# Loading the first quad's attention operands from inside the projection's program, with the projection unrolled

## What is computed

```python
q, k, v = split_heads(x @ Wq.T + bq), split_heads(x @ Wk.T + bk), split_heads(x @ Wv.T + bv)
q, k = rope(q), rope(k)
att = softmax(where(tril, q @ k.T / sqrt(16), -inf))
x = layernorm(x + (att @ v) @ Wo.T + bo)
h = silu(lin(x, w1)) * lin(x, w2)
h = gelu(lin(h, h1)); h = gelu(lin(h, h2))
out = layernorm(x + lin(h, w3))
```

## Time and profile before

| | |
|---|---|
| median of the three runs | 3086.01 us |
| profiled execution, its time | 3089.17 us |
| profiled execution, its span | 3087.4 us |
| TensorE matmuls busy | 2862.5 us (93%) |
| VectorE busy | 2063.2 us (67%) |
| ScalarE busy | 1302.7 us (42%) |
| GpSimd busy | 95.5 us (3%) |
| mean granted TensorE clock | 0.964 |

### The profile page before, as it was taken

The page is one execution under the profiler, slowest core; times in us unless marked ns, Lnnn a source line. Parts: engine busy times, 40 slices in busy tenths (PEclk is TensorE's granted clock), DMA queues, the critical chain, the costliest instruction groups (busy, mean ns, idle before and its releaser), DMA issues. The chain is left out here.

```text
span 3087.4 us, 40615 instructions
## 1 busy us (share of the span) xinstructions
PE 2862.5 (93%) x15648; PEld 1514.1 (49%) x15648; DVE 2063.2 (67%) x3638; ACT 1302.7 (42%) x2545; POOL 95.5 (3%) x122
## 2 busy tenths in 40 slices
PE   8949999999999989999999994699999994999998
PEld 4423333333333323333333332477777773888887
DVE  7979999887776779998877743655444432334333
ACT  0005666777777656667777772111111110010110
POOL 0030200020000200000000000000000000000000
PEclk9969999999999989999999997799999997999999
DMA  5541440034000440000000003211111004111200
GB/s 161 153 91 34 65 54 5 5 48 58 5 5 9 62 58 5 5 4 5 5 5 5 5 12 97 77 55 51 54 54 54 34 31 155 69 41 41 82 14 21
DMA packets 86620, 138.35 MB, mean 45 GB/s; under 512 B 27744, under 2 KB 57312, under 8 KB 83776
## 3 DMA queue, kind: packets, MB, share of 16 engines
q1 hardware_dynamic: 72352, 92.06, 9.2%
q0 software_dynamic: 5472, 23.34, 6.1%
q10 hardware_dynamic: 8640, 20.85, 2.1%
HBM read 85.22 MB, written 50.99 MB: 44 GB/s over the span
## 5 line engine op out<-in xcount | busy, mean ns | idle before, releaser
L506 DVE TENSOR_REDUCE at_segmax<-at_row 128x1 f32<-128x512 f32 (+3 forms) x2304 | 1330.3, 639 | 260.5 <-PE at_row L436 193.2
L559 ACT ACTIVATE at_probs<-at_key 128x512 f32<-128x512 f32 (+3 forms) x2304 | 1136.8, 567 | 546.8 <-PE at_key L452 376.8
L436 PE MATMUL at_row<-at_k_stack,at_q_stack 96*128 96x512 bf16 (+3 forms) x2304 | 814.7, 372 | 33.8 <-POOL at_values L362 28.7
L452 PE MATMUL at_key<-at_q_stack,at_k_stack 99*128 99x512 bf16 (+3 forms) x2304 | 814.3, 366 | 20.8 <-DMA at_q_stack<-maxima 11.7
L471 PE MATMUL at_o<-at_probs,at_values 128*32 128x512 f32 (+2 forms) x4608 | 574.7, 571 | 0.0
L436 PEld LDWEIGHTS at_row<-at_k_stack,at_q_stack 96*128 96x128 bf16 x2304 | 223.5, 99 | 595.1 <-DVE at_segmax L506 406.2
L452 PEld LDWEIGHTS at_key<-at_q_stack,at_k_stack 99*128 99x128 bf16 x2304 | 224.6, 98 | 279.2 <-ACT at_probs L559 129.4
L1012 PE MATMUL na_h<-na_h_h,na_h2w_h 128*128 128x512 f32 x512 | 203.5, 397 | 45.9 <-DVE na_h_l L1065 45.9
L1050 ACT ACTIVATE na_h3f<-na_h,na_hs 128x512 f32<-128x512 f32 x64 | 44.0, 688 | 442.0 <-PE na_h L1012 442.0
L746 PE MATMUL wi_f<-wi_h_h,wi_h1w_h 128*128 128x512 f32 x512 | 207.3, 405 | 10.4 <-DVE wi_h_l L877 10.4
L1012 PE MATMUL na_h<-na_h_h,na_h2w_l 128*128 128x512 f32 x512 | 203.2, 397 | 0.0
(11 more groups left out here) (108 smaller groups left out, 2520.9 us busy)
## 6 DMA issues: line engine op xcount, KB each, us to landing
hidden<-wi_h SPq DMA_DIRECT2D x64, 256.0 KB, 2.0
na_h2f<-hidden SPq DMA_DIRECT2D x8, 2048.0 KB, 8.6
at_q_stack<-q_parts POOLq DMA_DIRECT2D x72, 128.0 KB, 23.7
at_k_stack<-k_parts POOLq DMA_DIRECT2D x18, 512.0 KB, 28.4
outputs<-at_outs SPq DMA_DIRECT2D x32, 256.0 KB, 2.0
wi_o<-outputs SPq DMA_DIRECT2D x8, 1024.0 KB, 5.9
q_parts<-pr_parts SPq DMA_DIRECT2D x48, 128.0 KB, 1.9
k_parts<-pr_parts SPq DMA_DIRECT2D x48, 128.0 KB, 2.3
```

Of the source, the lines that this page charges most:

```text
L436: last = nc.tensor.matmul(bank[:, 0:w], qst[u][0:SROWS, c, h, i * P:(i + 1) * P], kst[u][0:SROWS, h, s * CH:s * CH + w], start=True, stop= ...
L452: last = nc.tensor.matmul(bank[:, q0:CH], kst[u][0:SROWS + PARTS, h, j * P:(j + 1) * P], qst[u][0:SROWS + PARTS, c, h, q0:CH], start=True, ...
L506: nc.vector.tensor_reduce(segmax[:, n % 2, h * TPC + i, s:s + 1], row_ps[r % RING_R][:, 0:w], op=ALU.max, axis=AX.X).then_inc(rows_taken, 1)
L559: nc.scalar.activation(probs[:, g % RING_P, h, q0:CH], key_ps[m % RING_K][:, q0:CH], ACT.Exp).then_inc(probs_ready, 1)
```

## The change

The tiles of the first quad (stacks, values, the float32 constants) move into a class `First`, allocated around both programs. In the projection:

* the hardware loops of ACT, PE, DVE and SP are written out for all eight chunks; the semaphores are no longer given their first counts ahead, the first waits are left out instead;
* SP issues the two constants first of all, and `load_first(n - 1)` in chunk n behind the stores of q and of the first half of the values. It first waits for all stores of chunks up to n - 1, and issues thirteen DMAs (six for the query stack, six for the key stack, one for the values of that chunk, 136 KB). `load_first(7)` stands at the end, behind the wait for all stores;
* POOL fills the ones and the pad of the first quad's tiles behind the staging tile.

In the attention SP has no loads of stacks left, POOL fills only the second buffer's pad and ones and then waits for chunk 7 of the first quad, and goes on to the loads of quad 1. PE waits for one pad, and for the values of quad 0 chunk by chunk.

```diff
         @block.gpsimd
         def _(pool):
             nc.gpsimd.memset(vals[:, :, :, :, :], 1.0).then_inc(v_ones, 1)
+            pool.wait_ge(v_ones, 1)
+            nc.gpsimd.memset(first.kst[SROWS:SROWS + PARTS, :, :], 1.0).then_inc(v_ones, 1)
+            pool.wait_ge(v_ones, 2)
+            nc.gpsimd.memset(first.vq[:, NT * QUAD * VW:], 0.0).then_inc(v_ones, 1)
+            pool.wait_ge(v_ones, 3)
...
         @block.sync
         def _(sp):
...
+            def load_first(n):
+
+                for s in range(2):
+                    sp.wait_ge(parts_stored[s], 96 * (n + 1))
+                    sp.wait_ge(v_stored[s], 32 * (n + 1))
+                for r, (qa, ka) in enumerate(TERMS):
+                    part = slice(r * HD, (r + 1) * HD)
+                    sp.dma_start(first.qst[part, n, :, :], q_v[qa, 0, :, n]).then_inc(first.loaded[n], 16)
+                    sp.dma_start(first.kst[part, :, n * CH:(n + 1) * CH], k_v[ka, 0, :, n]).then_inc(first.loaded[n], 16)
+                sp.dma_start(first.vq[:, n * TPC * QUAD * VW:(n + 1) * TPC * QUAD * VW],
+                             v_d[0, :, n].rearrange("p i e -> p (i e)")).then_inc(first.loaded[n], 16)
+
+            sp.dma_start(first.ident32[:, :], io["ident"]).then_inc(first.consts_loaded, 16)
+            sp.dma_start(first.mask32[:, :], io["mask"]).then_inc(first.consts_loaded, 16)
+            for n in range(NCH):
+                for i, dst in enumerate((qp_d, kp_d)):
+                    for half in range(DH):
+                        m = PAIRS * n + DH * i + half
+                        sp.wait_ge(parts_ready, 2 * m + 2)
+                        for a in range(PARTS):
+                            sp.dma_start(dst[a, half * P:(half + 1) * P, n, :],
+                                         parts[:, half, a, :]).then_inc(parts_stored[half], 16)
+                    sp.wait_ge(v_taken, 2 * n + i + 1)
+                    for j in range(2):
+                        sp.dma_start(v_d[:, :, n, 2 * i + j, :].rearrange("q p e -> p q e"),
+                                     vals[:, i, j, :, :].rearrange("p (q h) e -> p q (h e)", q=NQUAD)
+                                     ).then_inc(v_stored[i], 16)
+                    if n > 0 and i == 0:
+                        load_first(n - 1)
+            load_first(NCH - 1)
...
@@ attend, POOL
-            load_values(0, 0)
-            for u in range(2):
-                nc.gpsimd.memset(vq[u][:, NT * QUAD * VW:], 0.0).then_inc(pad_ready, 1)
-                pool.wait_ge(pad_ready, u + 1)
-                nc.gpsimd.memset(kst[u][SROWS:SROWS + PARTS, :, :], 1.0).then_inc(ones_ready[u], 1)
-                pool.wait_ge(ones_ready[u], 1)
-            pool.wait_ge(first_loaded[NCH - 1], 12 * 16)
+            nc.gpsimd.memset(vq[1][:, NT * QUAD * VW:], 0.0).then_inc(pad_ready, 1)
+            pool.wait_ge(pad_ready, 1)
+            nc.gpsimd.memset(kst[1][SROWS:SROWS + PARTS, :, :], 1.0).then_inc(ones_ready, 1)
+            pool.wait_ge(ones_ready, 1)
+            pool.wait_ge(first.loaded[NCH - 1], 13 * 16)
             load(1, 1)
             load_values(1, 1)
...
@@ attend, SP
-            load_first(0)
-            sp.dma_start(ident32[:, :], io["ident"]).then_inc(consts_loaded, 16)
-            sp.dma_start(mask32[:, :], io["mask"]).then_inc(consts_loaded, 16)
-            for c in range(1, FIRST_AHEAD):
-                load_first(c)
...
                             store_max(n)
-                            if n + FIRST_AHEAD < NCH:
-                                load_first(n + FIRST_AHEAD)
...
@@ attend, DVE
-            dve.wait_ge(consts_loaded, 32)
-            nc.vector.tensor_copy(ident[:, :], ident32[:, :]).then_inc(consts_ready, 1)
-            nc.vector.tensor_copy(mask[:, :], mask32[:, :]).then_inc(consts_ready, 1)
+            dve.wait_ge(first.consts_loaded, 32)
+            nc.vector.tensor_copy(ident[:, :], first.ident32[:, :]).then_inc(consts_ready, 1)
+            nc.vector.tensor_copy(mask[:, :], first.mask32[:, :]).then_inc(consts_ready, 1)
```

More of the change, by code:

```diff
@@ L54, with project @@
 EPS = 1e-5
-def project(nc, io, qp_d, kp_d, v_d):
+def project(nc, io, qp_d, kp_d, v_d, first):
     with ExitStack() as ctx:
@@ L119, in _ @@
             load(1, 1)
-            with act.Fori(0, NCH // 2 - 1) as it:
-                for u in range(2):
-                    act.wait_ge(v_ready, it * 4 + 2 * u + 2)
-                    act.wait_ge(pair_taken, it * 2 * PAIRS + PAIRS * (u + 1) + 2)
-                    load(u, it * 2 + (2 + u))
+            for n in range(2, NCH):
+                act.wait_ge(v_ready, 2 * (n - 2) + 2)
+                act.wait_ge(pair_taken, PAIRS * (n - 1))
+                load(n % 2, n)
         @block.gpsimd
@@ L133, in _ @@
             pe.wait_ge(weights_ready, 6)
[L134 to L150, removed]
+            for n in range(NCH):
+                u = n % 2
+                pe.wait_ge(x_loaded[u], 16 * (n // 2 + 1))
+                for i, (w, wr) in enumerate(((wq, wqr), (wk, wkr))):
+                    for half in range(DH):
+                        m = PAIRS * n + DH * i + half
+                        cols = slice(half * P, (half + 1) * P)
+                        if m >= 2:
+                            pe.wait_ge(pair_taken, m - 1)
+                        for bank, weight in ((main_ps[half], w), (rot_ps[half], wr)):
@@ L156, in _ @@
+                    for j in range(2):
+                        tile = slice((2 * i + j) * P, (2 * i + j + 1) * P)
+                        for c in range(DH):
+                            last = nc.tensor.matmul(v_ps[i][:, j, :], xt[:, u, c, tile], wv[:, c, :],
+                                                    start=(c == 0), stop=(c == DH - 1))
+                    last.then_inc(v_ready, 1)
         @block.vector
         def _(dve):
-            dve.sem_inc(pair_taken, 2)
-            dve.sem_inc(v_taken, 2)
@@ L176, in _ @@
             dve.wait_ge(v_ones, 1)
[L177 to L212, removed]
@@ L214, in _ @@
         @block.sync
         def _(sp):
[L216 to L232, removed]
@@ L233, in _ @@
[L233 to L235 removed]
+            q_v = qp_d.rearrange("a (q h d) n t -> a q d n h t", q=NQUAD, d=HD)
+            k_v = kp_d.rearrange("a (q h d) n t -> a q d n h t", q=NQUAD, d=HD)
+            def load_first(n):
[8 more added lines that the diff above has]
+                             v_d[0, :, n].rearrange("p i e -> p (i e)")).then_inc(first.loaded[n], 16)
@@ L284, in rows_before_keys, with __init__, sb, attend @@
     return before
-def attend(nc, io, qp_d, kp_d, v_d, max_d, o_d):
+class First:
+    def __init__(self, nc, ctx):
+        def sb(name, shape, dt=F32):
+            return ctx.enter_context(nc.sbuf_tensor("fi_" + name, shape, dt))
+        self.qst = sb("q_stack", [P, NCH, QUAD, CH], BF16)
+        self.kst = sb("k_stack", [P, QUAD, T], BF16)
+        self.vq = sb("values", [P, NT * QUAD * VW + 32 - VW])
+        self.ident32 = sb("ident32", [P, P])
+        self.mask32 = sb("mask32", [P, P])
+        self.loaded = [ctx.enter_context(nc.semaphore(f"fi_loaded{c}")) for c in range(NCH)]
+        self.consts_loaded = ctx.enter_context(nc.semaphore("fi_consts_loaded"))
+def attend(nc, io, qp_d, kp_d, v_d, max_d, o_d, first):
     blocks, rows, groups = attend_plan()
@@ L304, in sem @@
             return ctx.enter_context(nc.semaphore("at_" + name))
-        qst = [sb(f"q_stack{u}", [P, NCH, QUAD, CH], BF16) for u in range(2)]
-        kst = [sb(f"k_stack{u}", [P, QUAD, T], BF16) for u in range(2)]
-        vq = [sb(f"values{u}", [P, NT * QUAD * VW + 32 - VW]) for u in range(2)]
+        qst = [first.qst, sb("q_stack1", [P, NCH, QUAD, CH], BF16)]
+        kst = [first.kst, sb("k_stack1", [P, QUAD, T], BF16)]
+        vq = [first.vq, sb("values1", [P, NT * QUAD * VW + 32 - VW])]
         probs = sb("probs", [P, RING_P, QUAD, CH])
         outs = sb("outs", [P, 2, CH])
-        ident32 = sb("ident32", [P, P])
-        mask32 = sb("mask32", [P, P])
         ident = sb("ident", [P, P], BF16)
@@ L465, in values @@
                     pe.wait_ge(out_taken, n)
-                if j == 0 and n % NCH == 0:
+                if j == 0 and quad == 0:
+                    pe.wait_ge(first.loaded[c], 13 * 16)
+                elif j == 0 and n % NCH == 0:
                     pe.wait_ge(values_loaded[quad], 16)
@@ L484, in _ @@
                             if quad == 0:
-                                pe.wait_ge(first_loaded[c], 12 * 16)
+                                pe.wait_ge(first.loaded[c], 13 * 16)
                             elif m % NCH == 0:
@@ L1137, in build @@
     h2_d = nc.dram_tensor("hidden2", [NCH, P, FK, CH], F32, kind="Internal").ap()
-    project(nc, io, qp_d, kp_d, v_d)
-    attend(nc, io, qp_d, kp_d, v_d, max_d, o_d)
+    with ExitStack() as ctx:
+        first = First(nc, ctx)
+        project(nc, io, qp_d, kp_d, v_d, first)
+        attend(nc, io, qp_d, kp_d, v_d, max_d, o_d, first)
```

66 lines of the change are left out of this document (49 added, 17 removed).

## The result

The changed kernel takes 3142.49 us (median of four runs, 3138.1 to 3147.3), against 3086.09 before: a ratio of 1.0184, 95% interval 1.0167 to 1.0202, 56 us slower. The profiled execution has a span of 3141.2 us, 53.8 more than before. The forecast was 3112.3, in a range to 3132. The direction was right, the size (26 us) about half of what came.

What follows compares the result with a forecast made beforehand. DVE was taken to pace the projection and PE the attention, leaving the seam to win; +1.6 up to the attention's start, +21.2 for stalls and +3.5 for clock gave +26.3, 3112.3 us as median, range 3086 to 3132.

Steps and rivals of the forecast that it cites:

- Ones in the projection: Projection's start: POOL's new 13.75 us memset holds DVE's first tensor-scalar until about 15.6, +6.5 us.
- the rival that only casts are held: Projection's start: POOL's memset doesn't hold DVE's tensor-scalar, worth 6.5 us; 3081.1, or 3105.8 with the forecast's stalls; chance 0.07.
- Thirteen more DMAs: Projection, chunks 1 to 6: SP's extra loads delay the stores of k, DVE waits 0.7 us each time, +4.2 us.
- Unrolling: Projection: written-out loops shrink DVE's gap between L193 and L197, 16 times 0.06, -1 us (ends 0 and -2).
- The last chunk: Projection's end: last stores 0.8 us later, then thirteen more DMAs of 6.1 us while all engines wait, +6.9 us.
- The race of the casts: Attention's start: DVE's casts of the constants come before POOL's long memset (60 in 100), seam -15.0 us.
- Quad 1's wave: Blocks 0 and 1: POOL's load of quad 1 slows the maxima's trips; PE stalls 7.2 and 14.0, +21.2 us.
- the case of the forecast: Attention's start: DVE's casts go ahead of POOL's memset; whole kernel 3112.3 us, chance 0.44.
- the lost race: Attention's start: casts lose to POOL's memset; seam -7.6 instead of -15.0, stalls 15.3 and 8.5; 3122.3 us, chance 0.26.
- The rival by which 12 KB slip through: Attention's first blocks: DMA engines serve POOL's and SP's queues in turn, so no stall; 3087.6 us, chance 0.14.
- the stores land late: Projection: stores of k take as long as 6.4 us (or block 2 is caught too), +10 to +20, 3122 to 3132; chance 0.09.
- Clock: Attention, behind the larger stall on the maxima: PE's granted clock is lower, +3.5 us.

Runs made afterwards that it cites:

- ones_act: Changed kernel with the first key stack's ones written by ACT instead of POOL's memset in the projection: 3139.53 us.
- issues_alone: Changed kernel with SP's thirteen loads a chunk replaced by thirteen 256-byte DMAs, real loads at the attention's start: 3131.26 us, only the projection meant to be read.
- unroll_alone: Kernel before the change with nothing but the projection's loops written out: 3083.59 us against 3085.68.
- spread: Changed kernel with the same thirteen loads a chunk on SP's queue, cut into pieces of four, four and five between its stores: 3114.45 us.
- act_queue: Changed kernel with the first quad's loads issued by ACT's queue behind its own chunk loads, thirteen in a row, none on SP: 3112.19 us.
- quad1_late: Changed kernel with POOL issuing the loads of quad 1 only behind the last value unit of block 3: 3128.41 us.
- casts_first: Changed kernel with POOL waiting for both casts of the constants before its pad and ones in the attention: 3137.84 us.

## Why the prediction was right or wrong

- *Ones in the projection*, +6.5: measured 6.0, and the rival that only casts are held is refuted by the 7.00 us row and by ones_act.
- *Thirteen more DMAs*, +4.2: measured 26.8. **This is the step that failed.** The place, the six waits and the landing that makes DVE wait were right; the landing was mis-sized. I took the 3.1 us median of a 64 KB load behind its like, "since stores, not loads, wait here". The stores then had the thirteen loads and each other ahead of them, in five of the six chunks ACT's 1 MB beside them, and took 5.5 us in the median. The first decisive one took 6.5, about the 6.4 that I had put down as the upper end (worth +23 in all); in the next chunk they took up to 7.8. I had not asked what else is in flight when the burst goes out. Lateness alone cost 4.0 in issues_alone, near the 4.2, but by a shorter landing and a later issue than computed.
- *Unrolling*, -1: 1.4 us less in the stream of DVE (unroll_alone).
- *The last chunk*, +6.9: from the last cast of the projection to the attention's start it is now 15.97 us (198.51 to 214.48), before 8.29 (167.49 to 175.78): +7.7.
- *The race of the casts*, 60 in 100 for DVE: lost. The second cast was caught at 214.66, 0.01 us behind the memset's start, and the same is seen in spread, act_queue, issues_alone, quad1_late and ones_act. My figure for a cast, 0.08 us, was that of a cast that had been waiting; a fresh one takes 0.23, and the two don't fit into 0.17. The rival priced this at 10 us more; casts_first gives some 5.
- *Quad 1's wave*, +21.2 in the case of the forecast and 23.8 (15.3 and 8.5) in that of the lost race: measured 22.3 (16.4 and 5.9). The rival by which 12 KB slip through is refuted: a trip took 15.2 us beside POOL's wave, 1.4 without it. The Trainium skill, "DMA: Bandwidth & Descriptors", section "Queues, rings and completion order", has each engine change between its queues packet by packet, which was the reason for that rival. The trace doesn't bear out that this keeps a small transfer fast.
- *Clock*, +3.5: not separated. The attention from PE's first row unit on grew by 15.6 us. In the lists of waits PE's for the maxima's DMA grew by 21.5 (11.7 to 33.2, quad 3's included) and the turn's for DVE shrank by 7.1 (16.7 to 9.6); that leaves 1.2 us for the clock and all else. The granted clock was low there before too: 0.70 over the first 60 us from PE's first row unit, now 0.65.

With the lost race the sum was 3122.3; with 22.6 more for the stores it is 3144.9, against 3142.5. The stores alone would have put the forecast at 3134.9, outside the range; the lost race alone would not. The range reached to 3132 because I had given "the stores land late" and "the race is lost" as alternatives. Neither excludes the other, and both came.

## What to carry to other kernels

A transfer that somebody waits for should not go out late behind a burst of others: the price isn't the issue time (0.7 us a chunk here) but the landing behind the bytes that are in flight, by the sixth burst those of other queues too. Here it went away when the burst was cut up between the stores, and when the burst went to another queue, so that the stores were on time again. Moving work earlier moves what waited for it too: each long memset and each wave of loads that "had to wait anyway" needs a new place, found in the order of its neighbours' deadlines. When two unknown terms are independent, the range has to hold their sum.

## What was not expected of the hardware

A GpSimd memset's length goes with its columns and not with the partitions that it touches: 128 partitions by 1088 columns of float32 took 1.00 us, 3 partitions by 16384 columns of bfloat16 13.75. Until the end of the latter a DVE tensor-scalar was held (7.00 us instead of 0.43) as much as a cast (13.85 instead of 0.22).

A trip of 12 KB beside a wave of large loads takes 5.7 us when it starts 2 us behind the wave's first issue (casts_first), and 13 to 18 once the wave is full, if the wave lasts that long. Trips that began shortly before its end didn't outlast it: 3.2 us for the one that began at 288.82 in the changed kernel (the wave had landed at 291.9), 8.4 for the one at 443.02 in quad1_late (452.7).

Now and then one issue on SP takes much longer than the usual 0.43 us, at places that change from run to run: 1.87 us at 53.77 and 2.00 at 173.54 in the changed kernel, 2.29 at 101.11 in ones_act, 2.52 at 106.73 in casts_first. What it waited for stays open.
